# AdaLN block on one core: the second batch's x turned through DRAM, four row sets for six, loads in another order

## The reference

```
mod = (silu(c) @ wmod).reshape(2, 6, 1, 512)         # sa, ca, ga, sb, cb, gb
ga, gb = sign(g) * max(|g|, 0.25)                    # both gates are guarded
h = layernorm(x) * (1 + ca) + sa
x = x + ga * (h @ (weight * blockmask).T)            # blockmask: 32x32 blocks whose mask sums above 0
h = layernorm(x) * (1 + cb) + sb
x = x + gb * ((silu(h @ Wg.T * ag) * (h @ Wu.T * au)) @ Wd.T * ad)    # inner width 1376
```

## Time and profile before

| | |
|---|---|
| median of 3 runs | 178.93 us |
| the profiled execution | 178.75 us |
| its span, first to last instruction | 177.0 us |
| PE busy in the span | 169.0 us |
| DVE, ACT, POOL busy | 97.6, 82.2, 29.9 us |
| granted TensorE clock | 1.00 |

### The profile page before, as it was taken

One profiled execution on the slowest core, in us unless ns is written; L12 is line 12 of the kernel. 1 busy time (PEld: TensorE's weight loads), 2 busy tenths in 40 slices (PEclk: granted clock), 3 DMA queues, 4 the chain that ended last, 5 costly groups with the idle time before them and its releaser, 6 DMA issues.

```text
span 177.0 us, 2551 instructions
## 1 busy us (share of the span) xinstructions
PE 169.0 (95%) x899; PEld 127.5 (72%) x899; DVE 97.6 (55%) x195; ACT 82.2 (46%) x115; POOL 29.9 (17%) x40
## 2 busy tenths in 40 slices
PE   6789999898999999999999999999999999999992
PEld 6645445363548888788888888888888888888882
DVE  6864812887266998335555764328644124442574
ACT  3023230918998987833664445543345433352200
POOL 1442520194009440000000000005600000000000
PEclk9999999999999999999999999999999999999999
DMA  6999986999956800431300000000500000000014
GB/s 176 359 411 392 419 273 157 419 409 405 398 226 206 275 15 19 103 93 31 122 0 4 2 4 0 4 0 20 219 7 0 4 0 4 2 4 0 4 59 178
DMA packets 12581, 23.99 MB, mean 136 GB/s; under 512 B 2984, under 2 KB 5296, under 8 KB 12048
## 3 DMA queue, kind: packets, MB, share of 16 engines
q1 hardware_dynamic: 11008, 22.23, 35.3%
q10 hardware_dynamic: 1552, 1.46, 2.7%
HBM read 19.48 MB, written 2.10 MB: 122 GB/s over the span
## 4 chain that ended last, share of the span: by engine, by line
PE 76%; DMA 8%; SPq 6%; DVE 4%; issue 2%; ACT 1%; POOL 1%
PE bank L843 45%; PE bank L913 20%; PE bank L813 6%; DMA wffn<-in_w_down 5%; SPq L234 4%; DMA modw<-in_mod_ln 3%; PE bank L899 2%; PE bank L797 2%; DVE bns L518 1%; SPq L243 1%; PE bank L757 1%; DVE wffn L539 1%; SPq L276 1%; POOL rstd L318 0%; DVE xt L744 0%
## 5 line engine op out<-in xcount | busy, mean ns | idle before, releaser
L843 PE MATMUL bank<-ht,whi_gu 128*128 128x512 f32 x352 | 83.3, 390 | 0.0
L843 PEld LDWEIGHTS bank<-ht,whi_gu 128*128 128x128 f32 x352 | 65.5, 188 | 14.0 <-issue 0.6
L647 DVE SCALAR_TENSOR_TENSOR awork<-bank,scal,awork 128x512 f32<-128x512 f32 x22 | 16.5, 750 | 50.0 <-PE bank L843 48.6
L913 PE MATMUL bank<-whi_dn,in_split 128*128 128x512 f32 x148 | 37.1, 390 | 0.0
L478 ACT ACTIVATE awork<-bank,scal 128x512 f32<-128x512 f32 x22 | 15.2, 690 | 43.9 <-PE bank L843 43.8
L813 PE MATMUL bank<-awork,wffn 128*128 128x512 f32 x64 | 31.8, 610 | 0.8 <-ACT maskt L391 0.6
L913 PEld LDWEIGHTS bank<-whi_dn,in_split 128*128 128x128 f32 x148 | 27.7, 188 | 5.7
L425 ACT ACTIVATE whi_gu<-wffn 128x1024 fp32r<-128x1024 f32 x22 | 23.3, 1058 | 7.3 <-PE bank L843 7.3
L418 ACT ACTIVATE junk<-wffn 128x1536 uint8<-128x1536 uint16 x11 | 16.3, 1481 | 4.9 <-DMA wffn<-in_w_down 4.8
L813 PEld LDWEIGHTS bank<-awork,wffn 128*128 128x128 f32 x64 | 10.5, 191 | 9.4 <-issue 6.6
L656 DVE TENSOR_TENSOR in_split<-awork,in_split 128x512 fp32r<-128x512 f32 x21 | 16.5, 786 | 0.7
(11 more groups left out here) (70 smaller groups left out, 108.8 us busy)
## 6 DMA issues: line engine op xcount, KB each, us to landing
wffn<-in_w_gu SPq DMA_DIRECT2D x10, 512.0 KB, 10.0
wffn<-in_w_down SPq DMA_DIRECT2D x10, 256.0 KB, 11.2
xt<-in_x SPq DMA_DIRECT2D x8, 256.0 KB, 6.2
modw<-in_mod_ln SPq DMA_DIRECT2D x4, 512.0 KB, 7.1
modw<-in_mod_gate SPq DMA_DIRECT2D x2, 1024.0 KB, 9.9
modw<-in_mod_ln SPq DMA_DIRECT2D x2, 1024.0 KB, 9.5
maskt<-in_att_mask SPq DMA_DIRECT2D x4, 256.0 KB, 6.3
awork<-in_att_w SPq DMA_DIRECT2D x4, 256.0 KB, 7.2
```

Source lines behind the costliest of these rows:

```text
L647: dve.scalar_tensor_tensor(inner[:, s % 2, :], bank[gu_bank(s, 1)][:, :], scal[:, c, 1:2], silu_g[:, s % 2, :], ALU.mult, ALU.mult).then_i ...
L843: return pe.matmul(bank[gu_bank(s, u)][:, :], w, h, start=(k == 0 and part == 0), stop=(k == KT - 1 and part == 1))
L913: last = pe.matmul(bank[4 + t][:, :], h, w, start=(c == 0 and part == 0), stop=(c == C - 1 and part == 1))
```

## The change

1. The second batch's x goes over DRAM. Each of the four normalised tiles is written, once its `xn_ok` count is there, to a new DRAM tensor `turn` (256 KB each, runs of 512 B, from 128 partitions). SP then waits for all four and reads four slabs of 256 KB back (runs of 2 KB, into 32 partitions each). The 16 moves are gone, ACT issues none.
2. The row sets are four: feature block 0; blocks 1 and 2; block 3 with the first gate; the second layernorm with the second gate (twelve blocks as before). The number of 128-column blocks is 24 in both.
3. SP's load order: ln1 of blocks 1 and 2 come ahead of mask 1; half of ln2[0] is loaded before the read back and half after it; ln2[1] and the second gate follow without a wait between them.
4. The first batch's normalisation goes by halves of the columns, and modulations 0 and 3 are split into 128 columns (`h_first`) and the other 384.
5. DVE mixes `transpose_first` with `gate_linear`; ACT puts `copy_gate(0)` before modulation 4 and `copy_gate(1)` before modulation 5, and has one check in place of two before the copy of the last rows.
6. The flags are in three groups (chunks 0 to 3, 4 to 6, 7 to 10) instead of two, the checks at one per step.

```diff
-GROUPS = [(0, 5), (5, C)]
+GROUPS = [(0, 4), (4, C - HELD), (C - HELD, C)]
...
+            load_mask(0)
+            load_ln1(0)
+            load_att(0)
+            load_ln1(1)
+            load_ln1(2)
+            load_mask(1)
+            load_att(1)
...
             sp.dma_start(modw[:, 2, :, :], mod_gate[0]).then_inc(d_gate[0], 16)
+            for t in range(TT):
+                sp.wait_ge(xn_ok, XN_FIRST + t + 1)
+                sp.dma_start(turn[:, :, t * P:(t + 1) * P].rearrange("j p n -> p j n"),
+                             xq0[:, :, t * P:(t + 1) * P]).then_inc(d_turn_out, 16)
             sp.wait_ge(rows_done, 2)
-            sp.dma_start(modw[:, 0, :, :], mod_ln2[0]).then_inc(d_ln2[0], 16)
-            sp.wait_ge(xn_ok, 2 * TT)
-            for n in range(BY_SYNC):
-                move_first(sp, n)
-            sp.wait_ge(rows_done, 4)
+            load_ln2(0)
+            sp.wait_ge(d_turn_out, 16 * TT)
+            for j in range(GRP):
+                sp.dma_start(xb0[BLK * j:BLK * (j + 1), :, :],
+                             turn[j].rearrange("(i q) n -> q i n", q=BLK)).then_inc(d_turn[j], 16)
+            load_ln2(1)
+            sp.wait_ge(rows_done, 3)
             sp.dma_start(modw[:, 1, :, :], mod_ln2[1]).then_inc(d_ln2[1], 16)
-            sp.wait_ge(rows_done, KT + 1)
             sp.dma_start(modw[:, 2, :, :], mod_gate[1]).then_inc(d_gate[1], 16)
...
+                if n in FIRST_ALONE:
+                    part = slice(P, SEQ)
+                    act.activation(dst[:, 0:P], src[:, 0:P], ACT.Identity,
+                                   bias=modc[:, layer, k, 2 + b:3 + b],
+                                   scale=modc[:, layer, k, b:b + 1]).then_inc(h_first, 1)
...
             between = {
-                (0, 0): [lambda: rows_ln1(1)],
-                (0, 1): [lambda: columns_ln1(1), lambda: transposes(2)],
...
+                (0, 0): [rows_second],
+                (0, 1): [lambda: columns(1), lambda: mask_blocks(1)],
+                (0, 2): [lambda: transposes(2)],
+                (1, 0): [lambda: transposes(3)],
+                (1, 1): [lambda: mask_blocks(2)],
+                (2, 1): [lambda: mask_blocks(3), rows_third],
+                (2, 2): [lambda: columns(2)],
...
+                for g in range(1, len(GROUPS)):
+                    if s == GROUPS[g][0] - 1:
+                        flag_sum(g)
```

More of the change, by code:

```diff
@@ L201, in adaln_block @@
         d_blocks = [sem(f"d_blocks{j}") for j in range(P // BLK)]
-        d_turn = [sem(f"d_turn{i}") for i in range(GRP)]
+        d_turn_out = sem("d_turn_out")
+        d_turn = [sem(f"d_turn{j}") for j in range(GRP)]
         checked = sem("checked")
@@ L336, in _ @@
             inverse_deviation(0, 1)
-            for k in range(KT - 1):
-                mask_weights(k)
+            mask_weights(0)
+            mask_weights(1)
             inverse_deviation(1, 0)
             inverse_deviation(1, 1)
-            mask_weights(KT - 1)
+            mask_weights(2)
+            mask_weights(3)
             for b in range(NB):
@@ L520, in stats, with normalise_half @@
                 dve.bn_aggr(mv[:, q, t, :], bns[:, q, t, :]).then_inc(stats_ok, 1)
+            def normalise_half(half, tiles):
+                cols = slice(half * HALF, (half + 1) * HALF)
+                for t in tiles:
+                    if half == 0 and t % 2 == 0:
+                        dve.wait_ge(rstd_ok, t // 2 + 1)
+                        dve.wait_ge(stats_ok, t + 2)
+                    dve.tensor_scalar(xn[:, t, cols], xt[:, t, cols], mv[:, 0, t, 0:1], rstd[:, 0, t:t + 1],
+                                      ALU.subtract, ALU.mult).then_inc(xn_ok, 1)
             def normalise(q, tiles=range(TT)):
@@ L709, in _ @@
                         gate_linear(1, t)
-                if s == 4:
-                    flag_vector(1)
-                    read_flag(1)
+                for g, (first, _) in enumerate(GROUPS):
+                    if s == first - 1:
+                        flag_vector(g)
+                        read_flag(g)
                 ffn_inner(s)
@@ L749, in _, with mod_rows @@
         def _(pe):
-            def mod_rows(n, sources, dst):
-                if n == 0:
-                    pe.wait_ge(silu_c, 1)
-                each = BLOCKS[n] // len(sources)
-                for i in range(BLOCKS[n]):
+            def mod_rows(blocks, dst):
+                for i, (at, source) in enumerate(blocks):
                     for j in range(KT):
-                        last = pe.matmul(dst[BLK * j:BLK * (j + 1), 0:P], sc[:, j, i * BLK:(i + 1) * BLK],
-                                         sources[i // each](j)[:, i % each * P:(i % each + 1) * P],
-                                         start=(i == 0), stop=(i == BLOCKS[n] - 1))
+                        last = pe.matmul(dst[BLK * j:BLK * (j + 1), 0:P], sc[:, j, at * BLK:(at + 1) * BLK],
+                                         source(j), start=(i == 0), stop=(i == len(blocks) - 1))
@@ L773, in columns_ln1, with modw_block, rows_first @@
-            def columns_ln1(k):
-                pe.wait_ge(rows_copied, k + 1)
-                pe.wait_ge(keep_ok, k + 1)
-                columns(k % 2, bank[7])
+                return lambda j: m[:, (2 * j + v) * P:(2 * j + v + 1) * P]
+            def modw_block(slot, i):
+                return lambda j: modw[:, slot, j, i * P:(i + 1) * P]
+            def rows_first():
+                pe.wait_ge(silu_c, 1)
+                pe.wait_ge(d_ln1[0], 16)
+                mod_rows([(v, ln1_block(0, v)) for v in range(2)], bank[6])
@@ new lines, in rows_last, with columns @@
+            def rows_last():
+                pe.wait_ge(d_ln2[0], 32)
+                pe.wait_ge(d_ln2[1], 16)
+                pe.wait_ge(d_gate[1], 16)
+                pe.wait_ge(att_read, 3)
+                mod_rows([(KT * slot + i, modw_block(slot, i)) for slot in range(3) for i in range(KT)], bank[2])
+            def columns(n):
+                pe.wait_ge(rows_copied, n + 1)
+                if n == SETS - 1:
+                    pe.wait_ge(att_read, 4)
+                else:
+                    pe.wait_ge(keep_ok, [1, 1, KT][n])
+                    if n:
+                        pe.wait_ge(modc_ok, n)
+                dst = bank[3 if n == SETS - 1 else 7]
+                pe.transpose(dst[:, 0:P], rows[:, n % 3, :], ident[:, :]).then_inc(cols_done, 1)
```

228 lines of the change are left out of this document (109 added, 119 removed).

## The result

The changed kernel takes 182.82 us (median of 4 runs, 181.17 to 184.25) against 178.89 (178.44 to 179.33) for the kernel before on the same chip: ratio 1.0189, 95% interval 1.0097 to 1.0281. The forecast was 179.7 with a range up to 181.4, so it was wrong in size, not in sign. The run of 184.25 was in a slower state of the chip, and like such runs of the experiments it counts in the median and not in the ratio. The median of the other three is 182.02, and one of them, 181.17, lies inside the range. The four runs are far apart for this kernel, and they go with the mean granted clock: span 179.4 us at 0.990, 180.2 at 0.987, 181.8 at 0.979 (the profiled one, 183.62 us), 182.4 at 0.978.

The account below looks back on a forecast made before the run. PE, busy 169.0 of 177.0 us, bounds it through the feed-forward start: 31.85 + 21.5 = 53.35 against 52.97, +0.4; flags +0.35; +0.75 on 178.75 gives 179.5, plus 0.18 to the median: 179.7, range 177.6 to 181.4.

Parts of the forecast that it names:

- The end is the start of the feed-forward part plus a constant: From 52.97 us PE runs matmul after matmul, so earlier changes count only by moving that start.
- The opening is worth nothing: Batch one ends at about 30.5 instead of 31.9, but this 1.4 us is hidden behind the turn.
- Writes landed at 25.45: Turn's writes to DRAM: from 21.05, 3.1 us of data, passed at 24.15, landed 1.3 us later.
- The rival of the slow writes: Turn's 512 B runs take 4.5 us instead of 3.1, X = 33.25, total 181.1 us; chance 0.17.
- X: Time at which all of batch two's turned x has landed: 30.48 before, forecast at 31.85.
- Reads: 2.0 fixed and 4.4 of data: Turn's read back from DRAM, issued at 25.5: 2.0 us fixed, then 4.4 us at 240 GB/s into 32 partitions.
- First `linear` of batch two at X + 1.6: After the turn, block transpose 0.78 and modulation 0.78 us put PE's start at X + 1.6, as before.
- Five calls at 0.86: PE's first five `linear` calls of batch two take 0.86 us each, after which the row set comes at X + 5.9.
- a fall of the clock: The forecast fails if PE's new idle lowers its granted clock, 1.00 in every window shown; no size given.
- From X to the feed-forward part, 21.5: Batch two's path to the feed-forward start takes 21.5 us, against 22.5 before: the new order gives back 1.0.
- The wait of 0.7 for modulation 8: Modulation 8, behind checks of chunks 1 and 2, ends at X + 15.0 and makes the next turn wait 0.7 us.
- Flags, 0.35: The third flag group costs PE 0.35 us on the path: a 0.12 sum and `down` at 2.04 instead of 1.81.

Follow-up runs that it names:

- e7_write_runs: Changed kernel with the DRAM writes in runs of 2 KB instead of 512 B, all four after the last tile, batch two's output permuted; 183.11 us, ratio 1.0220.
- e4_read_wide: Changed kernel with the turn read back into all 128 partitions instead of 32, batch two's x permuted; 182.21 us, ratio 1.0201.
- e8_ln2_whole: Changed kernel with the 16 moves within SBUF of before and all of ln2[0] loaded ahead of them; 178.38 us, ratio 0.9960.
- e5_fill14: Changed kernel plus 14 identity matmuls filling PE's hole between batch one's last linear and batch two's first; 181.98 us, ratio 1.0164.
- e9_dram_whole: Changed kernel with 14 filler matmuls and all of ln2[0] ahead of the read back; 184.07 us, ratio 1.0265.
- e2_moves: Changed kernel with only the turn undone, back to the 16 moves within SBUF of before; 180.99 us, ratio 1.0134.
- e10_moves_9_7: Changed kernel with SBUF moves and all of ln2[0] ahead of them, nine moves on SP and seven on ACT instead of ten and six; 177.78 us, ratio 0.9919.
- e11_two_flags: Changed kernel with SBUF moves, all of ln2[0] ahead of them and two flag groups instead of three, first flag one call later; 178.93 us, ratio 0.9982.
- e3_turn_alone: Kernel before with only the turn sent over DRAM, half of ln2[0] on either side of the reads; 183.55 us, ratio 1.0236.
- e1_fill: Changed kernel plus 28 identity matmuls on PE between batch one's last linear and batch two's first; 183.00 us, ratio 1.0233.

## Why the prediction was wrong

By its own steps, on the profiled execution (183.62 us, 4.87 over that of before):

- *The end is the start of the feed-forward part plus a constant*: right. From that start to the end of the span are 124.5 us, 124.0 before; the difference is the flags.
- *The opening is worth nothing*: right, but for another reason. Batch one was to end at 30.5 and ends at 31.92, where the forecast had 31.9 for the kernel before: the weight loads stand idle 0.79 us ahead of 27.34 for a modulation, and PE 0.56 us ahead of the first gate's row set at 23.84, the gate having landed at 23.8. The gain that was to be hidden never came.
- *Writes landed at 25.45*: wrong by 1.25. The data took 3.48 us of all engines (301 GB/s) where the term had 3.1 (338 GB/s, from rows whose writes go out in other shapes): 0.4. The landing came 2.1 us behind the data instead of 1.3: 0.8, the tail of the last tenth. The rival of the slow writes came true by its mark (landing after 26.5, X = 33.25) and not by its size, which was 4.5 us of data; that X agrees with it is luck. Runs of 512 B do cost something, 0.7 us against 2 KB (e7_write_runs), but not that much.
- *Reads: 2.0 fixed and 4.4 of data*: nearly right, 6.76 for 6.4. From issue to first packet 0.96, to the last 4.93, to the landing 0.87; 227 GB/s at full share against the 240 taken. The Trainium skill's page on the SBUF (SBUF — State Buffer, Door 1: The DMA port swizzle) gives about 218 for 32 partitions; for these loads from DRAM the packets give 227, and 321 with 128 partitions (e4_read_wide), so its rule holds here too.
- *First `linear` of batch two at X + 1.6*: 1.83.
- *Five calls at 0.86*: the step that failed most, in this execution. They took 7.43 us, 3.13 more than at full clock. The prediction named a fall of the clock as what would refute it, and said in the same text that PE would idle 2 to 3 us; it gave that neither a price nor a chance. The slow stretch, 34.3 to 41.1 us, begins 1.0 us ahead of these calls and covers some three and a half of them.
- *From X to the feed-forward part, 21.5*: 23.85, less the clock's 3.13 it is 20.7; e8_ln2_whole has 20.9 at full clock. The wait of 0.7 for modulation 8 was not there. Chunk 0 landed at X + 9.1 for X + 8.3, the second gate at X + 7.0 for X + 6.3.
- *Flags, 0.35*: nearly right (0.12, and 2.14 for 1.81, so 0.45).

The sum: 0.75 forecast, + 1.61 for X, + 3.13 for the clock, - 0.78 for the order, + 0.1 for the flags is 4.81, of 4.87. The other runs have clocks of 0.987 and 0.990, so less of their time can be the clock, and the median is 3.9 over before. Without the clock the same sum would be 1.7 over before; e5_fill14, which holds the clock, still measures 3.0 (181.98 against 178.98). What stands between, by its profiled execution, is an X 0.5 us later still and the second thing the prediction missed: the second gate lands at 41.3 (X + 7.3) instead of 36.15, and PE waits 1.16 us for it. The prediction had the gate within 0.4 us of its need, by 415 GB/s from X - 1.3 on, and gave that no price. From 34 us on the queue does reach 387 to 426 GB/s, but all that follows the turn starts late with it. The turn takes the DMA time from the weights as well: its packets fill all 16 engines for 3.48 and 4.62 us, where those of the moves of before, also 1.05 MB, fill them for 4.0.

So two steps failed, and of the three microseconds by which the median missed, the record doesn't say how much is each: the clock, put at nothing (3.13 us in the profiled execution), and X at 31.85, which came at 33.5 to 35.8 in the changed kernel, its two filler versions and e9_dram_whole, with the gate behind it.

What stays open: why the last tenth of a turn's packets takes so long (the writes' 1.9 us in the changed kernel, the reads' 0.7 there, 1.5 in e7_write_runs and 2.1 in e9_dram_whole); no run has the writes without at least half of ln2[0] behind them, so that this load is what holds them back, or they it, is an untested rival. Open too is how X moves in the 9 and 7 version. X varies between executions with the SBUF moves too (29.9 to 33.4 in e2_moves, e8_ln2_whole and e10_moves_9_7; and in e11_two_flags, whose loads and moves are those of e8_ln2_whole, DVE's transpose starts at 30.60 where it starts at 31.93 there), so the order of loads around them is not the only reason.

## What to carry to other kernels

A round trip over DRAM costs two landings, one behind the other, and the data twice, each way at its own rate (301 GB/s out in runs of 512 B, 227 back into 32 partitions, here); price both, and the loads behind it in the queue as well. When a forecast contains a new idle stretch of PE of some us in front of dense work, write down what that work costs at 1.2 GHz (at most the rows at full clock, doubled; here 7.43 us for 4.3) and give the case a chance of its own. Filler matmuls can hold the clock, but measure one first, and look at what the next wait is: here holding it was worth little. And when a large edit is slower, undo its parts one by one: here ScalarE's order alone (177.94) and the whole change with SBUF moves, nine of them on SyncE, and ln2[0] whole (177.78) are both faster than the kernel before.

## What the runs showed of the hardware

- The granted clock after an idle stretch of PE: 1.00 after 1.61 us (e8_ln2_whole); 0.50 in some stretch behind 2.44 us (e4_read_wide), 3.37 (the changed kernel), 4.25 (e3_turn_alone) and 4.27 us (e7_write_runs); but 1.00 behind 2.55 us (e10_moves_9_7) and 2.74 us (e9_dram_whole). So the length of the idle stretch alone does not settle it. Nor is it the same in every run: the changed kernel's have 0.978 to 0.990 over the span, and one of e4_read_wide's 1.00.
- A float32 matmul of the identity by itself (128x128) took 0.22 us in the filler, since each stands as two matmuls in the record (28 give x56); a `transposes` matmul is one record and takes 0.11 (0.44 for four). The filler was sized by the latter, hence its overshoot in e1_fill.
- Writes from 128 partitions to DRAM, at full share: 294 to 303 GB/s with runs of 512 B in six executions, 377 with runs of 2 KB in one. The Trainium skill's page DMA: Bandwidth & Descriptors (Specifications) has the line rate from 512 B on. This case does not bear that out: runs of 512 B stay well under those of 2 KB, and under the 415 of the loads.
- Reads from DRAM in runs of 2 KB, at full share: 227 GB/s into 32 partitions, 321 into 128, and the DMA share reads about 1 in both.
